# Attention heads of 32 rows, two of them in a 64-row tile of TensorE, with the scores of one half beside the maxima of the other and the keys brought through DRAM

## The reference

```python
q, k, v = xn @ Wq + bq, ctx @ Wk + bk, ctx @ Wv + bv       # layer 0 with biases, layer 1 with 8x8 blocks
scores = einsum('bhqd,bhkd->bhqk', q, k) * scale            # 16 heads, 100 queries, 1444 keys
scores = where(mask == 0, -inf, scores)                     # layer 1 masked per key, layer 3 by length, layer 0 not
out = softmax(scores) @ v @ Wo
```

## Time and profile before

| | us |
|---|---|
| median of 3 runs | 6744.95 (6734.53 to 6745.65) |
| the profiled execution | 6736.52 |
| its span in the trace | 6734.7 |
| PE busy | 5947.1 |
| DVE busy | 4732.6 |
| ACT busy | 3471.3 |
| POOL busy | 1972.7 |

### The profile page before, as it was taken

One profiled execution on the slowest core, in us unless ns is written; L12 is line 12 of the kernel. 1 busy time (PEld: TensorE's weight loads), 2 busy tenths in 40 slices (PEclk: granted clock), 3 DMA queues, 4 the chain that ended last, 5 costly groups with the idle time before them and its releaser, 6 DMA issues. The chain is left out here.

```text
span 6734.7 us, 123692 instructions
## 1 busy us (share of the span) xinstructions
PE 5947.1 (88%) x42776; PEld 4044.1 (60%) x42776; DVE 4732.6 (70%) x12652; ACT 3471.3 (52%) x5250; POOL 1972.7 (29%) x1415
## 2 busy tenths in 40 slices
PE   6999999969897999999999956768498799999996
PEld 4666666659894555555555545645388466566653
DVE  6878777867676666666666676634577777777775
ACT  3666666655553444444444433423255466666664
POOL 2222222224453222222222122334255222222220
PEclk9999999989997999999999977878699799999998
DMA  3333333220002333333333132356332333232321
GB/s 75 77 78 73 72 72 75 63 68 21 21 21 68 81 77 81 78 79 75 76 79 75 35 68 52 60 157 183 98 118 81 82 72 71 67 69 68 69 67 25
DMA packets 200964, 492.88 MB, mean 73 GB/s; under 512 B 31689, under 2 KB 135318, under 8 KB 199162
## 3 DMA queue, kind: packets, MB, share of 16 engines
q1 hardware_dynamic: 200386, 485.47, 29.5%
HBM read 270.18 MB, written 2.25 MB: 40 GB/s over the span
## 5 line engine op out<-in xcount | busy, mean ns | idle before, releaser
L850 PE MATMUL a_max<-a_stack,a_qblk 96*100 96x482 f32 (+1 forms) x4608 | 2003.5, 455 | 114.3 <-DVE a_mx L671 35.7
L550 ACT ACTIVATE a_probs<-a_scores 128x800 f32<-128x800 f32 (+1 forms) x1536 | 1281.3, 838 | 1019.0 <-PE a_scores L867 656.9
L863 PE MATMUL a_scores<-a_qblk,a_stack 128*128 128x400 f32 (+1 forms) x4608 | 1378.7, 372 | 8.1 <-POOL a_qblk L455 2.7
L665 DVE CUSTOM_DVE_ANT_0 a_dump<-a_max,a_mqf 100x482 f32<-100x482 f32 (+1 forms) x1536 | 978.5, 657 | 426.4 <-PE a_max L850 395.6
L850 PEld LDWEIGHTS a_max<-a_stack,a_qblk 96*100 96x100 f32 x4608 | 767.2, 167 | 745.1 <-issue 205.6
L671 DVE CUSTOM_DVE_ANT_0 a_dump<-a_max,a_penq 100x482 f32<-100x482 f32 (+1 forms) x1536 | 955.6, 657 | 280.9 <-PE a_max L850 261.7
L657 DVE TENSOR_REDUCE a_mx<-a_max 100x1 f32<-100x482 f32 (+1 forms) x1536 | 941.4, 654 | 257.6 <-PE a_max L850 239.8
L879 PE MATMUL a_pv<-a_probs,a_v_aug 128*32 128x200 f32 x18432 | 1051.8, 340 | 3.4 <-ACT a_probs L548 2.1
L863 PEld LDWEIGHTS a_scores<-a_qblk,a_stack 128*128 128x128 f32 (+1 forms) x4608 | 840.4, 186 | 185.6 <-issue 52.7
L1165 POOL TENSOR_TENSOR f_hb<-f_hb,f_wb 128x400 f32<-128x400 f32 x560 | 655.8, 1185 | 965.1 <-DVE f_hb L1413 490.2
L548 ACT ACTIVATE a_probs<-a_scores,a_kbias 128x800 f32<-128x800 f32 (+1 forms) x768 | 697.5, 926 | 413.6 <-PE a_scores L863 413.4
(11 more groups left out here) (302 smaller groups left out, 8471.7 us busy)
## 6 DMA issues: line engine op xcount, KB each, us to landing
a_stack<-a_khi SPq DMA_DIRECT2D x768, 180.5 KB, 3.4
a_ctxT<-in_ctxT_dram SPq DMA_DIRECT2D x128, 722.0 KB, 8.5
a_stack<-a_klo SPq DMA_DIRECT2D x384, 180.5 KB, 3.5
f_wb<-weights_by_token SPq DMA_DIRECT2D x24, 1600.0 KB, 10.7
f_wb<-weights_by_token SPq DMA_DIRECT2D x64, 400.0 KB, 6.3
a_ctxn<-in_ctxn_dram SPq DMA_DIRECT2D x32, 704.0 KB
a_mt_i<-in_mask1T_dram SPq DMA_DIRECT2D x32, 600.0 KB, 6.9
a_mq_i<-in_mask_dram SPq DMA_DIRECT2D x32, 564.1 KB
```

Source lines behind the costliest of these rows:

```text
L550: act.activation(out_, in_, ACT.Exp, scale=scale).then_inc(sc_free, 1)
L665: nc.vector.tensor_tensor_reduce(dump[:, k % 2, 0:n], src, mqf[:, b % 2, o:o + n], 1.0, -3.0e38, ALU.mult, ALU.max, out_).then_inc(mx_free, 1)
L850: pe.matmul(to[0:S, 0:n], qblk[0:96, b % 2, HALF * h + head, :], stack[0:96, b % 2, g, o:o + n], start=True, stop=True).then_inc(mx_full, 1)
L863: ins = pe.matmul(out_, stack[:, b % 2, 2 * h + g, kt * D:kt * D + r], qblk[:, b % 2, HALF * h + 4 * g:HALF * h + 4 * g + 4, :].rearrange( ...
```

## The change

Each head gets 32 rows of its own: rows 0 and 1 for the negated maximum (high, low), row 2 for the key penalty of a3, rows 8 to 31 for three times the 8 columns (key high, key low, key high; query high, high, low). Two heads share 64 rows, one half of 8 heads is rows 0 to 63 in four groups, the other rows 64 to 127. The maxima of one head are a 64-row matmul with the other head's 32 query rows at zero. The scores are four matmuls (two heads, 200 moving columns) in place of two. `LEAD` is 24, and the halves change places with each batch (`half_of`), so that the maxima matmuls of a unit are always on the 64 rows that its score matmuls are not on; `max, score, score, max, score, score` is the order in a unit. In a1 the two penalty matmuls (128 rows) go first in a unit and open the accumulation.

Keys: two DMAs write khi and klo to DRAM (`k_store`), and four (a3: six) per half bring them to the rows (`stack_load`). Queries: POOL makes the parts with five instructions (`q_parts`), the bias of q (a0) and the constant row of a3 come in as a one-row matmul `q_row` behind each of the four. The maxima's high and low parts are made on POOL (`neg_parts`), turned in four matmuls, copied by DVE (`neg_rows`) and brought to their rows by two DMAs (`neg_load`). In a3 the key penalty is a row of the stack, so that DVE's reduction is the plain one of a0 and the exponential has no bias. The positions of the jobs change: K at units 1 and 3 (13 and 15 before), V at 7 and 9 (9 and 11), q at 10 (18), neg at 4 and 15 (9 and 21).

```diff
-LEAD = 16
+LEAD = UNITS
+ROWS = 32
-        OUT_AT, CONCAT_AT, WO_AT, NEG1_AT, U_AT, Q_AT, NEG0_AT = 2, 5, 8, 9, 13, 18, 21
-        V01_AT, V2_AT, K0_AT, K12_AT = 9, 11, 13, 15
+        OUT_AT, NEG1_AT, CONCAT_AT, WO_AT, Q_AT, U_AT, NEG0_AT = 2, 4, 5, 8, 10, 13, 15
+        K0_AT, K12_AT, V01_AT, V2_AT = 1, 3, 7, 9
+        def half_of(b, j):
+            return (b + j) % 2
...
         @block.sync
+            def k_store(b):
+                sp.wait_ge(klo_ready, b + 1)
+                if b >= SLOTS:
+                    stack_there(sp, b - SLOTS, 0)
+                    stack_there(sp, b - SLOTS, 1)
+                for part, src in enumerate((khi, klo)):
+                    sp.dma_start(k_dram[b % SLOTS, :, :, :, part, :, :].rearrange("t g s i k -> (t g s) i k"),
+                                 src[:, :].bitcast(F32)).then_inc(k_out, 16)
+            def stack_load(b, j):
+                h = half_of(b, j)
+                sp.wait_ge(k_out, 32 * (b + 1))
+                scored(sp, b - 2, j)
+                for r in range(2):
+                    at, from_ = ROWS * (2 * h + r), k_dram[b % SLOTS, h, :, r]
+                    sp.dma_start(stack[at + 8:at + 24, b % 2, :, 0:KEYS].bitcast(F32),
+                                 from_.rearrange("g p i k -> (p i) g k")).then_inc(stack_in[b % 2][h], 16)
+                    sp.dma_start(stack[at + 24:at + 32, b % 2, :, 0:KEYS].bitcast(F32),
+                                 from_[:, 0].rearrange("g i k -> i g k")).then_inc(stack_in[b % 2][h], 16)
+                    if lens is not None:
+                        sp.dma_start(stack[at + 2:at + 3, b % 2, :, 0:KEYS].bitcast(F32), ...)
+            def neg_load(b, j):
+                taken(sp, "neg", 2 * b + j)
+                for r in range(2):
+                    sp.dma_start(qst[at:at + 2, b % 3, :, r, :].bitcast(F32), nsb[at:at + 2, :, :].bitcast(F32))
...
         @block.gpsimd
             for b in range(B):
-                if b + 1 < B:
-                    q_spread(b + 1, 1)
-                    gone_keys(b + 1)
-                neg_spread(b, 1)
                 if b + 2 < B:
                     k_low(b + 2)
-                    q_low(b + 2)
-                    q_spread(b + 2, 0)
                 if b + 1 < B:
-                    neg_spread(b + 1, 0)
+                    gone_keys(b + 1)
+                if b + 2 < B:
+                    q_parts(b + 2)
+                if b + 1 < B:
+                    neg_parts(b + 1, 0)
+                    neg_parts(b + 1, 1)
...
         @block.tensor
             def q_proj(b):
                 for g in range(GROUPS):
-                    ins = pe.matmul(to[0:96, g * S:(g + 1) * S], wq[:, g, :], xnT[:, b * S:(b + 1) * S],
-                                    start=True, stop=True)
+                    ins = pe.matmul(to[:, g * S:(g + 1) * S], wq[:, g, :], xnT[:, b * S:(b + 1) * S],
+                                    start=True, stop=q_row is None)
+                    if q_row is not None:
+                        ins = pe.matmul(to[:, g * S:(g + 1) * S], q_row[:, g, :], ones_row[:, :], start=False, stop=True)
+            def neg_turn(b, j):
+                for g in range(GROUPS):
+                    ins = pe.matmul(to[at:at + 2 * ROWS, g * S:(g + 1) * S], nmsp[:, h, g, :].bitcast(F32), ...)
             def max_mm(k):
-                pe.matmul(to[0:S, 0:n], qblk[0:96, b % 2, HALF * h + head, :], stack[0:96, b % 2, g, o:o + n],
-                          start=True, stop=True).then_inc(mx_full, 1)
+                at = 2 * ROWS * half_of(b, j)
+                pe.matmul(to[0:S, 0:n], qst[at:at + 2 * ROWS, b % 3, g, r, :],
+                          stack[at:at + 2 * ROWS, b % 2, g, o:o + n], start=True, stop=True).then_inc(mx_full, 1)
+            def score_mm(b, u, g):
+                ins = pe.matmul(to[:, g // 2, g % 2 * 2 * S:(g % 2 + 1) * 2 * S],
+                                stack[at:at + 2 * ROWS, b % 2, g, kt * D:(kt + 1) * D],
+                                qst[at:at + 2 * ROWS, b % 3, g, :, :].rearrange("p r s -> p (r s)"), ...)
+            def penalty_mm(b, u):
+                to = slot("exp", UNITS * b + u)
+                for i in range(2):
+                    pe.matmul(to[:, i, 0:4 * S].rearrange("p (h s) -> p h s", h=4), identb[:, :],
+                              bc(pen[:, b % 2, u % KT, :], 1, 4), start=True, stop=False)
...
                     g = UNITS * b + u + LEAD
+                    if mask is not None:
+                        penalty_mm(b, u)
                     max_mm(2 * g)
-                    score_mm(b, u)
+                    score_mm(b, u, 0)
+                    score_mm(b, u, 1)
+                    max_mm(2 * g + 1)
+                    score_mm(b, u, 2)
+                    score_mm(b, u, 3)
...
-                max_mm(2 * g + 1)
```

More of the change, by code:

```diff
@@ L403, in _ @@
             maskt_load(0)
+            if lens is not None:
+                sp.wait_ge(gone_row_ready, 1)
+                sp.dma_start(gone_dram, gone_row[:, :].bitcast(F32)).then_inc(gone_out, 16)
+            k_store(0)
             stack_load(0, 0)
             stack_load(0, 1)
+            maskq_load(1)
+            k_store(1)
             stack_load(1, 0)
-            maskq_load(1)
+            ctx_load(2)
             maskt_load(1)
-            ctx_load(2)
+            neg_load(0, 0)
             for b in range(B):
@@ L412, in _ @@
                     stack_load(b + 1, 1)
+                neg_load(b, 1)
                 if b + 2 < B:
                     maskq_load(b + 2)
-                    maskt_load(b + 2)
+                    k_store(b + 2)
                 if b + 3 < B:
@@ new lines, in neg_parts @@
+            def neg_parts(b, j):
+                h = half_of(b, j)
+                pool.wait_ge(nm_ready, 2 * b + j + 1)
+                if b > 0:
+                    full(pool, "neg", 2 * (b - 1) + 1 - j)
+                cols = nmsp[:, h, :, :].rearrange("p g (r w) -> p g r w", w=ROWS)
+                nm_ = nm[:, h, :].rearrange("p (g r) -> p g r", r=2)
+                step(pool.tensor_copy(cols[:, :, :, 0], nm_))
+                pool.tensor_tensor(cols[:, :, :, 1], nm_, cols[:, :, :, 0].bitcast(F32),
+                                   ALU.subtract).then_inc(negm_ready, 1)
@@ L545, in exps @@
                 in_ = p_slot("exp", at)[0:rows, :, 0:4 * S]
-                if lens is not None:
-                    apart(act, passed["act"])
-                    act.activation(out_, in_, ACT.Exp, bias=kbias[0:rows, b:b + 1, kt], scale=scale).then_inc(sc_free, 1)
-                else:
-                    act.activation(out_, in_, ACT.Exp, scale=scale).then_inc(sc_free, 1)
+                act.activation(out_, in_, ACT.Exp, scale=scale).then_inc(sc_free, 1)
             def pen_make(b):
@@ L587, in _ @@
                         em_make(b, 1)
-                    if u == Q_AT + 2 and b + 2 < B:
-                        q_round(b + 2)
+                    if u == NEG0_AT + 2 and b + 1 < B:
+                        em_make(b + 1, 0)
                     exps(b, u)
@@ L656, in reduce_max @@
-                if not special:
+                src, out_ = p_ring("max", k)[0:S, 0:n], mx[:, half_of(b, j), g, r, c:c + 1]
+                if b > 0 and k % (2 * KT) == 0:
+                    dve.wait_ge(nm_ready, 2 * (b - 1) + 1 - j + 1)
+                if mask is None:
                     nc.vector.tensor_reduce(out_, src, AX.X, ALU.max).then_inc(mx_free, 1)
@@ L758, in _ @@
                     g = UNITS * b + u + LEAD
-                    if u == 3 and b + 1 < B:
-                        mask_rows(b + 1)
                     maxima(g, 0)
+                    maxima(g, 1)
                     if b > 0:
@@ L830, in u_proj @@
                 ins.then_inc(mx_full, 1)
-            def neg_turn(b, h):
-                to = ring("neg", 2 * b + h)
-                pe.wait_ge(negm_ready, 2 * b + h + 1)
-                pe.matmul(to[96:128, 0:S], nmsp[:, h, :].bitcast(F32), ident[0:S, 0:S],
-                          start=True, stop=True).then_inc(mx_full, 1)
+            def neg_turn(b, j):
+                to = ring("neg", 2 * b + j)
+                h = half_of(b, j)
+                at = 2 * ROWS * h
+                pe.wait_ge(negm_ready, 2 * b + j + 1)
+                for g in range(GROUPS):
+                    ins = pe.matmul(to[at:at + 2 * ROWS, g * S:(g + 1) * S], nmsp[:, h, g, :].bitcast(F32),
+                                    ident[0:S, 0:S], start=True, stop=True)
+                ins.then_inc(mx_full, 1)
@@ L859, in score_mm @@
+            def penalty_mm(b, u):
+                if u == 0:
                     pe.wait_ge(pen_ready, b + 1)
                 to = slot("exp", UNITS * b + u)
-                for g in range(2):
-                    out_ = to[0:r, g, 0:4 * S]
-                    ins = pe.matmul(out_, stack[:, b % 2, 2 * h + g, kt * D:kt * D + r],
```

(5 more changed lines are left out.)

335 lines of the change are left out of this document (165 added, 170 removed).

## The result

Slower: 6956.32 us (median of 4 runs, 6946.99 to 6964.35) against 6740.34 (4 runs, 6734.53 to 6745.65) for the kernel before; ratio 1.032, 95% interval 1.0302 to 1.0338. Forecast were 6573 us and faster; the time lies inside the range, on the other side of no change.

A forecast was written before the change was run, and what follows sets the result against it. PE was taken to set the pace in all three phases. Terms of -105 (a0), -177 (a3), +71 (a1) and +47 us (phase edges) gave -164 on 6736.5: 6573 us, range 6400 to 7320.

The forecast's parts named there:

- the stage: Maxima and score matmuls of each unit: both chains run at once, 0.45 us instead of 0.81, -8.6 us a batch.
- loads within a group overlap the matmuls ahead of them: Score weight loads: forecast as hidden; the rival, not hidden within one row group, gave 7310 us, chance 0.06.
- rounded-f32 matmuls of 200 columns aren't dear: Scores: forecast 0.11 us each; the rival, short rounded-f32 matmuls dear at 0.33 us, gave 8540 us, chance 0.11.
- the way in and out of a shape: PE entering and leaving the 64-row shape: 0.2 us a round trip, +2.0 us a batch in a0 and a3, +4.8 in a1.
- the wait in a1: PE stands while ACT's `pen_make` waits for POOL's `gone_keys`: +4.7 us a batch; rival that it is absent: 6430 us, chance 0.08.
- `q_proj`'s own time: `q_proj` in a0 and a3: one-row matmuls between its 128-row pairs make it 2.8 us instead of 0.8, +2.0 us a batch.
- DVE stays under PE's 37, hence costs nothing: a0 and a3: DVE has 33 us of work a batch, below PE's 37, so it adds no time.
- The edges: Phase starts and ends: longer `LEAD` and 9.5 us each for the open DMA trip, +17.6, +13.1, +16.8, together +47 us.
- loads that don't overlap across row groups: Rival for maxima and scores: weight loads of the two row groups run in turn, 0.61 us, 6930 us in all, chance 0.15.
- scores beside maxima: Sign in a0's timeline: score matmuls start within 0.02 us of a maxima matmul; 0.2 us behind would prove the prediction wrong.
- a0's unit: Sign: PE's unit in a0 near 1.55 us; the prediction is wrong if it isn't between 1.45 and 1.65.
- Another named sign: PE's waits: the prediction is wrong if DVE or a DMA of the stack ends them.

The follow-up runs named there:

- pen_late_q_bias: Changed kernel with a1's `pen_make` called at unit 10 instead of 5, and q's bias added in DVE's copy instead of by one-row matmuls: 6520.22 us, ratio 0.9667.
- pen_late: Changed kernel with only a1's `pen_make` called at unit 10 instead of unit 5: 6738.26 us, ratio 1.000 to the kernel before.
- q_bias_dve: Changed kernel without `q_proj`'s one-row matmuls in a0 and a3; DVE adds the bias column while copying q: 6731.10 us, ratio 0.9989.
- one_row_last: Changed kernel with `q_proj`'s four one-row matmuls behind its four 128-row matmuls instead of between them: 6797.42 us, ratio 1.0083.
- both_half_reduce: pen_late_q_bias with DVE's reductions of the maxima over only the first half of each chunk: 6419.05 us, ratio 0.9517.

## Why the prediction was wrong, by its own steps

The sum was 383 us too low: 6956 against 6573. Between the two profiled executions it is 392 (+228 measured, -164 forecast): 299 in 31 batches of each phase, 93 in their starts and ends. Three steps failed: the granted clock had no term, DVE below PE's total was taken to cost nothing, and the starts of the phases were priced too low.

**Right: the stage.** The two chains run at once, loads of both row groups start together, loads within a group overlap the matmuls ahead of them (scores start at 614.00, 614.20, 614.31 and 614.42), and rounded-f32 matmuls of 200 columns aren't dear. The Trainium skill (same page, section on packing small matmuls) has loads overlap matmuls only where the row group differs; this trace disagrees once more. A unit between two other jobs took 0.99 us in the kernel before (601.61 to 602.60 below) and takes 0.62: -0.37 for -0.36 forecast. The stage itself is 0.51 and not 0.45, since the first pair's load is in the open, but behind another job it was in the open before too.

```profile
600.58 0.38 PE L850 MATMUL a_max<-a_stack,a_qblk 96*100 96x482 f32 x1
...
601.61 0.46 PE L850 MATMUL a_max<-a_stack,a_qblk 96*100 96x482 f32 x1
...
602.60 1.02 PE L879 MATMUL a_pv<-a_probs,a_v_aug 128*32 128x200 f32 x16
```

**Too low: the way in and out of a shape,** 0.3 us and not 0.2. Timeline of PE in a0 of pen_late_q_bias, a job of two K matmuls and what comes ahead and behind:

```profile
602.57 0.37 PE L892 MATMUL a_max<-a_stack,a_qst 64*100 64x482 f32 x1
...
602.90 1.07 PE L843 MATMUL a_scores<-a_ctxT,a_wk 128*128 128x480 f32 x2
603.90 0.46 PE L892 MATMUL a_max<-a_stack,a_qst 64*100 64x482 f32 x1
```

The job starts 0.33 us behind the maxima matmul, where 0.22 is the rule in the kernel before (600.58, then L810 at 600.80 in the earlier trace rows): 0.11 for the way in. Then it takes 1.00 us, where such matmuls in the kernel before start 0.41 us apart, 0.82 for two: 0.18 more. For V's eight it is 0.10 and 0.28. `q_proj`'s eight, without the one-row matmuls, went from 0.63 to 1.07 us; the forecast read 0.8 for the 0.63.

**Right: the wait in a1,** place and size (4.7 forecast, 4.9 measured, pen_late). a1's batch came out at 56.1 us for 56.4. But 1.8 us of slow clock hang on the wait too, and they are covered by something cheaper: without the wait 51.7 us were forecast and pen_late has 49.4. It is the unit. Before and in pen_late, from its first matmul to the next job:

```profile
2817.21 0.46 PE L850 MATMUL a_max<-a_stack,a_qblk 96*100 96x482 f32 x1
...
2818.55 0.89 PE L879 MATMUL a_pv<-a_probs,a_v_aug 128*32 128x200 f32 x16
```

```profile
2806.76 0.51 PE L912 MATMUL a_scores<-a_pen,a_identb 128*128 128x400 bf16 x2
2807.20 0.46 PE L891 MATMUL a_max<-a_stack,a_qst 64*100 64x482 f32 x1
...
2807.82 3.40 PE L866 MATMUL a_max<-a_v_aug,a_gone 128*100 128x144 f32 x24
```

1.34 us became 1.06, -0.28 where stage and round trip were to give -0.36 + 0.2 = -0.16. If all 24 units did as well, it would be 2.9 us a batch, an estimate from these two; the dearer ways in and out take some of it back. Half of the units come behind values, which have 128 rows like the penalty, so the penalty's way in is not a new one there.

**The first step that failed: the sum has no term for the granted clock.** I read 1.00 in the earlier trace rows and carried it over. The change adds two stretches behind which it falls to 0.5: `q_proj` in a0 and a3, and the wait in a1. The pieces in a0: q_bias_dve takes 3.85 us; 2.12 of them is `q_proj`'s own time (3.19 - 1.07 in the median, from its first start to the next job's; 2.0 forecast), and the other 1.7 goes with the slow clock behind it, 1.7 in a3 too. one_row_last shows that the falls go when the shape changes once instead of eight times. In a1 it is the 1.8 above. Over 31 batches these are about 160 us, by subtraction.

**The second: "DVE stays under PE's 37, hence costs nothing".** With the clock at 1.00 and no one-row matmuls the sum gives 37.1 - 2.0 = 35.1 us a batch in a0 and a3; measured are 38.4 and 38.0. PE and DVE are coupled through three slots, unit by unit. Six times a batch two units stand one right behind the other, and there the fourth maxima matmul finds no free slot. Timeline of PE in pen_late_q_bias, third and fourth:

```profile
623.22 0.38 PE L892 MATMUL a_max<-a_stack,a_qst 64*100 64x480 f32 x1
...
623.90 0.46 PE L892 MATMUL a_max<-a_stack,a_qst 64*100 64x480 f32 x1 [0.30 <-DVE a_mx L701]
```

It starts 0.67 us after the third on average in place of 0.22: 0.45 x 6 = 2.7 us a batch, in a0 and in a3. With half the reduction it is still 0.44 (both_half_reduce), which gives back 0.23 x 6 = 1.4, and 1.3 were measured in a0; so that run shows half of what the ring costs. Of the 3.3 and 2.9 us between sum and measurement this leaves 0.6 and 0.2 for the dearer ways in and out and for what offsets them.

**The edges: +140 us measured from the first K matmul to the first update of x, +47 forecast for all edges.** From the first K matmul to the first reduction it is 13.8, 11.3 and 16.1 us more (9.5 forecast). From the first reduction to the first exponential it is 26.5, 27.2 and 24.1 more (12 forecast). The rows at 127.55 and 135.83 show what was forgotten: at the start nothing covers the second half's `stack_load` (2.46 us) and `neg_load` (7.57 us), which the forecast counted as hidden and, at the start, not at all. These two intervals explain 55 of the 93 us; the rest wasn't separated.

**The rivals.** The one nearest in time, loads that don't overlap across row groups (6930 us), was false: their loads start together at 614.00. No mechanism that decided stood among the rivals. By what the trace was to show, scores beside maxima and the idle stretch in a1 came; a0's unit is 42.2/24 = 1.76 us, outside 1.45 to 1.65, which was named as a sign that the prediction fails. Another named sign came as well: PE's weight loads for the maxima waited 60.5 of 400 us for DVE's reductions (changed kernel, 600 to 1000 us).

## What to carry to other kernels

Read the granted clock of the stretch that a change touches, and ask what the change does to PE's work there: here nearly every stretch in which PE stood still for 5 us or changed its shape every 0.39 us was paid twice, once itself and once in the 3.4 to 10.2 us (a few times 14 to 17) at 1.2 GHz behind it. An engine that is busy 83% of the time (DVE in pen_late_q_bias, a0: 165.31 of 200 us) isn't free: look at the few units in which it has to keep up without a pause (here 2.7 us a batch). Group matmuls of one shape, even where each belongs to another result: four one-row matmuls in a row cost 1.1 us, four between full ones 2.1 us and the clock. A large change can hide its gain behind small side effects; undo these one at a time before judging it (two edits turned +3.2% into -3.3%).
